# Layer-1 cross attention: keys and queries turned once and spread over the partitions by DMA, weighing in bursts

## The reference, cut to what matters

```python
q = split_heads(layernorm(latents) @ Wq)                 # [b, 16, 1024, 64]
k, v = split_heads(concat(latents, context) @ Wkv)       # [b, 16, 1101, 64]
q, k = rmsnorm(q) * qn_g, rmsnorm(k) * kn_g              # over the 64 of a head
attn = softmax(q @ k.T, masked)                          # [b, 16, 1024, 1101]
out = (attn @ v) @ Wout + bout                           # added to the residual
```

## Time and profile before

| | |
|---|---|
| median of 3 runs | 2421.39 us (2419.66 to 2424.4) |
| the profiled execution | 2413.85 us, span 2411.9 us |
| TensorE matmuls busy | 2050.4 us, 85% of the span |
| VectorE, ScalarE, GpSimd busy | 1344.9, 925.7 and 768.4 us (56%, 38%, 32%) |
| granted TensorE clock, mean | 0.925 |
| first and last exponential of layer 1's attention | 723.3 and 1943.7 us |

### The profile page before, as it was taken

One profiled execution on the slowest core, in us unless ns is written; L12 is line 12 of the kernel. 1 busy time (PEld: TensorE's weight loads), 2 busy tenths in 40 slices (PEclk: granted clock), 3 DMA queues, 4 the chain that ended last, 5 costly groups with the idle time before them and its releaser, 6 DMA issues. The chain is left out here.

```text
span 2411.9 us, 37994 instructions
## 1 busy us (share of the span) xinstructions
PE 2050.4 (85%) x12524; PEld 1558.7 (65%) x12525; DVE 1344.9 (56%) x3047; ACT 925.7 (38%) x1778; POOL 768.4 (32%) x730
## 2 busy tenths in 40 slices
PE   5889539997158999999999999999999934899993
PEld 3568535665046777777777877777777723567672
DVE  4371236665615777776777777767777725112223
ACT  3443202222124555544555555545554511222220
POOL 2200002332155444443454434544454100222220
PEclk9999759999559999999999999999999975899997
DMA  5512451111200000000000000000000055111113
GB/s 184 159 58 86 160 183 35 46 43 37 93 20 1 8 8 8 1 8 8 8 1 8 8 7 8 1 9 8 8 7 1 1 203 184 46 33 33 34 32 115
DMA packets 55772, 114.65 MB, mean 48 GB/s; under 512 B 8817, under 2 KB 41263, under 8 KB 53563
## 3 DMA queue, kind: packets, MB, share of 16 engines
q1 hardware_dynamic: 44987, 89.77, 10.6%
q0 software_dynamic: 8320, 20.65, 3.0%
q10 hardware_dynamic: 2304, 2.10, 0.3%
HBM read 79.90 MB, written 32.41 MB: 47 GB/s over the span
## 5 line engine op out<-in xcount | busy, mean ns | idle before, releaser
L1633 DVE TENSOR_REDUCE a_part_peak<-a_slot 128x1 f32<-128x512 f32 (+1 forms) x512 | 353.3, 728 | 124.3 <-PE a_slot L1467 121.4
L1467 PEld LDWEIGHTS a_slot<-a_KHL,a_QHL 128*128 128x128 f32 x1536 | 271.3, 190 | 176.8 <-issue 127.3
L1467 PE MATMUL a_slot<-a_KHL,a_QHL 128*128 128x512 f32 (+1 forms) x1536 | 342.9, 359 | 26.3 <-DVE a_probT L1663 12.8
L1492 PE MATMUL a_po<-a_probT,a_V 128*64 128x256 f32 (+1 forms) x2304 | 304.6, 390 | 3.3 <-DVE a_OT L1693 2.5
L1590 ACT ACTIVATE a_prob<-a_slot,a_npeak 128x1024 f32<-128x1024 f32 x256 | 284.5, 1111 | 1.3 <-DVE a_npeak L1635 1.2
L1663 DVE COPY a_probT<-a_slot 128x640 f32<-128x640 f32 x256 | 210.6, 823 | 102.8 <-PE a_slot L1476 92.7
L1476 PE MATMUL a_slot<-ident,a_prob 128*128 128x128 f32 x2048 | 265.4, 273 | 0.0
L1476 PEld LDWEIGHTS a_slot<-ident,a_prob 128*128 128x128 f32 x2048 | 231.7, 141 | 8.4
L1416 PE MATMUL a_side<-a_W,a_latT 128*128 128x128 f32 x1536 | 204.5, 289 | 21.0 <-issue 9.1
L1492 PEld LDWEIGHTS a_po<-a_probT,a_V 128*64 128x64 f32 (+1 forms) x2304 | 145.7, 136 | 92.1 <-issue 43.9
L1416 PEld LDWEIGHTS a_side<-a_W,a_latT 128*128 128x128 f32 x1536 | 188.2, 200 | 23.2 <-issue 9.5
(11 more groups left out here) (322 smaller groups left out, 3203.3 us busy)
## 6 DMA issues: line engine op xcount, KB each, us to landing
m_up<-_L_ffn_gate_up_proj_dram SPq DMA_DIRECT2D x8, 1024.0 KB
m_up<-in_L_ffn_W_dram SPq DMA_DIRECT2D x8, 1024.0 KB
m_down<-in_L_ffn_W_dram SPq DMA_DIRECT2D x8, 1024.0 KB
a_prob_dram<-a0p_zeros SPq DMA_DIRECT2D x4, 1632.0 KB, 10.6
a_dist_dram<-a_dist SPq DMA_DIRECT2D x4, 1632.0 KB, 8.2
a_band_prob<-a_prob_dram SPq DMA_DIRECT2D x4, 1632.0 KB, 6.7
a_W<-in_L_xattn_Wpair_dram SPq DMA_DIRECT2D x17, 384.0 KB, 3.1
m_bup<-_L_ffn_gate_up_bias_dram SPq DMA_DIRECT2D x1, 4096.0 KB
```

Source lines behind the costliest of these rows:

```text
L1467: ins = t_.matmul(out[:, lo:hi], q, KHL[:, pair.parity, h, part, lo:hi], start=part == 0, stop=part == 1)
L1492: ins = t_.matmul(po_t[h * D1:(h + 1) * D1, :], V[0:rows, pair.parity, j, h, :], probT[0:rows, gi % 2, j, h, :], start=j == PARTS[0][0], s ...
L1633: v.tensor_reduce(part[:, i:i + 1], slot[u % 2][:, lo:hi], AX.X, ALU.max).then_inc(part_peaked, 1)
```

## The change

- Keys and queries are scaled in place, once, and each tile is transposed once with both heads on its 128 rows. The high and low parts stand in new tiles `KT` and `QT`, head 0 on partitions 0 to 63, head 1 on 64 to 127.
- Four DMA transfers a pair copy `KT` to its places in `KHL`, and four for each half of the queries copy `QT` to `QHL`; each goes from 64 partitions to 64. SP issues them behind the weights' load. The scores wait for them.
- There are 12 pieces, in the units of `PIECE_OF`. In even units a piece stands behind the unit's transposes, in odd units at the unit's start.
- Weighing stands in odd units only, in parts of four and five tiles.
- VectorE now copies the first four tiles of the turned exponentials and ScalarE the other five, which waits for all nine.
- The bounds of the norms stand at the end of units 5 and 9.

```diff
-PARTS = [[8, 0], [1, 2], [3, 4], [5, 6, 7]]
-PIECES = ["Ka", "Kb", "c", "Qa", "Qb", "Va", "Vb", "K0a", "K0b", "K1a", "K1b", "Kc", "Q0a", "Q1a", "Q0b", "Q1b"]
-QUERY_TURNS = ["Q0a", "Q1a", "Q0b", "Q1b"]
-COPIED = ["Ka", "Kb", "c", "Qa", "Qb", "Va", "Vb"] + QUERY_TURNS
-SPLIT = [p for p in PIECES if p not in COPIED]
+PARTS = [[8, 0, 1, 2], [3, 4, 5, 6, 7]]
+PIECES = ["Ka", "Kb", "c", "Qa", "Qb", "Kta", "Va", "Ktb", "Ktc", "Qta", "Vb", "Qtb"]
+QUERY_TURNS = ["Qta", "Qtb"]
+SPLIT = ["Kta", "Ktb", "Ktc"]
+TURNED = SPLIT + QUERY_TURNS
+COPIED = [p for p in PIECES if p not in SPLIT]
+BOUND_AT = (5, 9)
+PIECE_OF = dict(zip([0, 2, 3, 4, 6, 7, 8, 9, 10, 11, 12, 13], PIECES))
...
-        kdup = sb("kdup", [P, KT_TILES, 2, 2, D1])
-        qdup = sb("qdup", [P, S, 2, 2, D1])
+        KT = sb("KT", [P, 2, KEYS], F32R)
+        QT = sb("QT", [P, 2, SEQ], F32R)
...
+            def spread_keys(pair):
+                sp.wait_ge(dve_freed, count(pair, "Ktc", SPLIT))
+                for h in range(2):
+                    for half in range(2):
+                        sp.dma_start(KHL[half * D1:(half + 1) * D1, pair.parity, h, :, 0:KEYS].bitcast(F32),
+                                     KT[h * D1:(h + 1) * D1, :, :].bitcast(F32)).then_inc(k_spread, 16)
+            def spread_queries(pair, k):
+                sp.wait_ge(qlow, pair.g * 2 + (k + 1))
+                for h in range(2):
+                    for part in range(2):
+                        sp.dma_start(QHL[part * D1:(part + 1) * D1, pair.parity, h, k * BANK:(k + 1) * BANK].bitcast(F32),
+                                     QT[h * D1:(h + 1) * D1, part, k * BANK:(k + 1) * BANK].bitcast(F32)).then_inc(q_spread[k], 16)
             def body(pair):
                 if not isinstance(pair.g, int) or pair.g + 2 < BATCH * PAIRS:
-                    sp.wait_ge(filled, count(pair, PIECES[-1], PIECES))
+                    sp.wait_ge(filled, count(pair, "Vb", PIECES))
                     load_weights((pair.hp + 2) % PAIRS if isinstance(pair.g, int) else pair.hp + 2, pair.parity)
+                spread_keys(pair)
+                for k in range(2):
+                    spread_queries(pair, k)
...
+                    x = nat[:, :, :].rearrange("p t (h d) -> p (t h) d", h=2)
+                    g_.tensor_tensor(x, x, inv[:, :].unsqueeze(2).to_broadcast([P, 2 * tiles, D1]), ALU.mult).then_inc(scaled, 1)
+                for k, step in enumerate(QUERY_TURNS):
+                    cols = slice(k * BANK, (k + 1) * BANK)
                     if not first:
-                        pool.wait_ge(filled, count(Pair(pair.g - 1, 0, 0, 0), last, PIECES))
-                    for h in range(2):
-                        src = nat[:, :, h * D1:(h + 1) * D1]
-                        scale = inv[:, :].rearrange("p (t h) -> p t h", h=2)[:, :, h:h + 1].to_broadcast([P, tiles, D1])
-                        for d in range(2):
-                            ins = g_.tensor_tensor(dup[:, :, h, d, :], src, scale, ALU.mult)
-                    ins.then_inc(scaled, 1)
-                for k, step in enumerate(QUERY_TURNS):
-                    lo = BANK if step.endswith("b") else 0
+                        pool.wait_ge(q_spread[k], n * 64)
                     pool.wait_ge(act_freed, count(pair, step, COPIED))
-                    q = QHL[:, pair.parity, int(step[1]), lo:lo + BANK]
-                    g_.tensor_tensor(q, qgam[:, k % 2, :], one[:, :].to_broadcast([P, BANK]), ALU.mult).then_inc(qhigh, 1)
-                    pool.wait_ge(qhigh, n * 4 + (k + 1))
-                    g_.tensor_tensor(q[D1:, :], qgam[D1:, k % 2, :], q[D1:, :], ALU.subtract).then_inc(qlow, 1)
-                    pool.wait_ge(qlow, n * 4 + (k + 1))
+                    g_.tensor_tensor(QT[:, 0, cols], qgam[:, k, :], one[:, :].to_broadcast([P, BANK]), ALU.mult).then_inc(qhigh, 1)
+                    pool.wait_ge(qhigh, n * 2 + (k + 1))
+                    g_.tensor_tensor(QT[:, 1, cols], qgam[:, k, :], QT[:, 0, cols], ALU.subtract).then_inc(qlow, 1)
...
-                    pe.wait_ge(dve_freed, count(pair, "Kc", SPLIT))
-                if u % 2 == 0 and t % HALF == 0:
-                    pe.wait_ge(qlow, count(pair, QUERY_TURNS[h + t // HALF * 2], QUERY_TURNS))
+                    pe.wait_ge(k_spread, (pair.g + 1) * 64)
+                if u % (UNITS // 2) == 0:
+                    pe.wait_ge(q_spread[u // (UNITS // 2)], (pair.g + 1) * 64)
...
-                    if after:
-                        piece(after, PIECES[u])
+                    if after and u % 2 == 1 and PIECE_OF.get(u):
+                        piece(after, PIECE_OF[u])
                     pe.wait_ge(exped, pair.g * UNITS + (u + 1))
                     if u % 2 == 1 and two_before[0]:
                         project_outputs(*two_before, u // 2 % 2)
                     if u % 4 == 2 and one_before[0]:
                         turn_sums(*one_before)
                     turn(pair, u)
-                    if one_before[0]:
-                        weigh(*one_before, u % 4)
+                    if after and u % 2 == 0 and PIECE_OF.get(u):
+                        piece(after, PIECE_OF[u])
+                    if one_before[0] and u % 2 == 1:
+                        weigh(*one_before, u // 2 % 2)
...
-            def copy_first(pair, u):
-                act.wait_ge(turned, (pair.g * UNITS + u) * 3 + 2)
+            def copy_rest(pair, u):
+                one_before, two_before = group_before(pair, u, 1), group_before(pair, u, 2)
+                if u % 2 == 1 and two_before[0]:
+                    act.wait_ge(added, (two_before[0].g * GROUPS + two_before[1]) * 2 + (u // 2 % 2 + 1))
+                if u % 4 == 2 and one_before[0]:
+                    act.wait_ge(r_out, one_before[0].g * GROUPS + (one_before[1] + 1))
+                act.wait_ge(turned, (pair.g * UNITS + u) * 3 + 3)
                 t, h = tile_head(u)
-                a_.activation(probT[:, u // 4 % 2, 0:HALF, h, u % 2 * P:(u % 2 + 1) * P],
-                              slot[u % 2][:, 0:HALF * P].rearrange("p (t q) -> p t q", q=P), ACT.Copy).then_inc(probT_act, 1)
+                a_.activation(probT[:, u // 4 % 2, HALF:KT_TILES, h, u % 2 * P:(u % 2 + 1) * P],
+                              slot[u % 2][:, HALF * P:KT_TILES * P].rearrange("p (t q) -> p t q", q=P), ACT.Copy).then_inc(probT_act, 1)
...
-            def bound(pair, step):
-                if step in ("Qb", "K0b"):
-                    j = int(step == "K0b")
+                    lo = {"Kta": 0, "Ktb": BANK, "Ktc": SEQ}[step]
+                    hi = min(lo + BANK, KEYS)
+                    v.tensor_tensor(KT[:, 1, lo:hi], side[:, 0:hi - lo], KT[:, 0, lo:hi], ALU.subtract).then_inc(dve_freed, 1)
+            def bound(pair, j):
                     var = (kvar, qvar)[j]
                     dve.wait_ge(summed, pair.g * (2 * FOLDS) + (j + 1) * FOLDS)
                     sums = square[:, 0:(KT_TILES, S)[j], :].rearrange("p t (h d) -> p (t h) d", h=2)
                     v.tensor_scalar(var[:, :], sums[:, :, 0], D1 * 1e-16, None, ALU.max).then_inc(bounded, 1)
-            def copy_rest(pair, u):
-                dve.wait_ge(turned, (pair.g * UNITS + u) * 3 + 3)
+            def copy_first(pair, u):
+                dve.wait_ge(turned, (pair.g * UNITS + u) * 3 + 2)
                 t, h = tile_head(u)
-                v.tensor_copy(probT[:, u // 4 % 2, HALF:KT_TILES, h, u % 2 * P:(u % 2 + 1) * P],
-                              slot[u % 2][:, HALF * P:KT_TILES * P].rearrange("p (t q) -> p t q", q=P)).then_inc(probT_dve, 1)
+                v.tensor_copy(probT[:, u // 4 % 2, 0:HALF, h, u % 2 * P:(u % 2 + 1) * P],
+                              slot[u % 2][:, 0:HALF * P].rearrange("p (t q) -> p t q", q=P)).then_inc(probT_dve, 1)
...
-                    if after:
-                        piece(after, PIECES[u])
+                    if after and u % 2 == 1 and PIECE_OF.get(u):
+                        piece(after, PIECE_OF[u])
                     if u % 2 == 1 and two_before[0]:
                         dve.wait_ge(turned, (pair.g * UNITS + u) * 3 + 1)
                         add_outputs(*two_before, u // 2 % 2)
                     if u % 4 == 2 and one_before[0]:
                         dve.wait_ge(turned, (pair.g * UNITS + u) * 3 + 1)
                         copy_sums(*one_before)
-                    copy_rest(pair, u)
+                    copy_first(pair, u)
                     row_sum(pair, u)
                     if u % 4 == 3:
                         invert(pair, u // 4)
                     nxt = ahead(pair, u, 2)
                     if nxt[0]:
                         peak(*nxt)
-                    if after:
-                        bound(after, PIECES[u])
+                    if after and u % 2 == 0 and PIECE_OF.get(u):
+                        piece(after, PIECE_OF[u])
+                    if after and u in BOUND_AT:
+                        bound(after, BOUND_AT.index(u))
```

(38 more changed lines are left out.)

11 lines of the change are left out of this document (3 added, 8 removed).

## The result

The changed kernel takes 2657.13 us in the median of 4 runs (2653.92 to 2667.2), against 2420.52 for the kernel before: a ratio of 1.0975, 95% interval 1.0947 to 1.1003. I forecast 2598, in 2490 to 2655: slower was right, and so was the place of each wait, but the time lies 59 us above the forecast and 2 us above the range.

The account below looks back on a forecast made before the run. TensorE's own work was taken to bound the stage. A pair gained +11.3 us from removed work, three waits and lower clock: 170 over 15 hand-overs plus 7 for the last, from 2421 to 2598 us; range 2490 to 2655.

Parts of the forecast that it names:

- wait for the keys' scale: TensorE in unit 7, at the keys' transposes, waits for GpSimd's scaling: 2.76 us a pair.
- wait for the queries' scale: TensorE in unit 11, at the queries' transposes, waits for GpSimd's scaling: 3.21 us a pair.
- wait for the spread: TensorE at unit 14's score waits for SP's DMA transfers: 6.4 us a pair, less 0.15 of idle absorbed.
- parts 1 to 3: TensorE's halved transposes, remaining work and added idle: a pair takes 73.30 us without the waits, 2.52 less than before.
- part 6: TensorE's steps after the long DMA wait run at lower clock: 1.61 us a pair; nothing for waits under 3.5.
- rival (d): Every TensorE wait halves the clock too: 3.2 us a pair on top, 2646 us; chance 0.08.
- part 5: Key and query transfers queue behind SP's weights load; 2.779 MB at 240 GB/s delays unit 14's score 6.4 us.
- Parts 4 and 3: TensorE waits 2.76 and 3.21 us for GpSimd's scaling; lost cover around ScalarE's copy, units 10 and 14, adds 1.83 idle.
- Part 2: TensorE's work after: 71.47 us a pair; the old pair's 2.29 of small waits, chiefly for the copy, all go.
- Part 7: The ends: last pair, without pieces, costs 7 us more; prologue nothing net.
- Rival (c): Faster: removed work decides if TensorE's three waits total under 2.1 us a pair; 2390 us with none; chance 0.09.

Follow-up runs that it names:

- the 2372 us kernel: The kernel with both edits, small key piece copied on ScalarE before the exponentials and split on VectorE before the peaks: 2372.22 us, ratio 0.9819.
- The filled kernel: The changed kernel, waits kept, TensorE turning the identity 18 times before each scale wait and 56 before the spread wait: 2607.27 us, ratio 1.0779.
- the first experiment: The changed kernel, with SP sending keys and first half of queries when ready, before waiting for Vb and loading weights: 2507.83 us, ratio 1.0368.
- the early bounds: The changed kernel, with the norms bounded at the end of units 4 and 8 instead of 5 and 9: 2560.08 us, ratio 1.0584.
- 2348 us: The 2372 us kernel, with weighing of units 9 to 15 in three parts and four parts in the last pair: 2348.07 us, ratio 0.9680.
- the kernel with both edits: The changed kernel, with the spread sent ahead of the weights and the bounds in units 4 and 8: 2406.2 us, ratio 0.9949.

## Why the prediction was right in kind and short in size

I set the terms a pair against a middle pair of the trace after:

| term | forecast | measured | from |
|---|---|---|---|
| work and idles without the waits | 73.30 | 72.3 | the pair of the 2372 us kernel, parts 1 to 3 |
| wait for the keys' scale | 2.76 | 2.78 | 1520.63 + 1.16 to 1524.57 |
| wait for the queries' scale | 3.21 | 2.8 | scaling took 1.90 and not 2.06, unit 10 0.2 longer |
| wait for the spread | 6.25 | 7.7 | turn 14 to score 9.71; 2.04 without the wait |
| lower clock | 1.61 | 6.9 | below |
| sum | 87.1 | 92.5 | the trace: 92.6, 1481.40 to 1574.00, score behind the spread to the next |

**The step that failed is part 6**, and with it the sentence "For waits under 3.5 I add nothing". I had one passage behind a wait of 7.51, priced two steps of it, and let the short waits go free; they stood only in rival (d), at 0.08. What the rows after show: behind the keys' wait (2.6) projection, turn and weighing take 0.72, 2.05 and 2.67, where 0.43, 1.07 and 2.31 are normal: 1.6. Behind the queries' wait, by the same steps and the transposes (0.89): 2.6. Behind the spread's, the score 2.13, the projection 0.99, the turn 2.06, the weighing 2.58, where 1.16, 0.51 (it stands behind a score here), 1.07 and 2.31 are normal: 2.7. The turns stand wholly at the lower level of 1.2 GHz, against 2.4 elsewhere (granted clock 0.50 and 1.00); in some of the other steps the clock changes. Over the whole trace such passages stand behind the keys' wait in 13 of 15 pairs (21 in all), behind the queries' in all 15 (35) and behind the spread's in all 14 (36): 6.1 in the mean of the 15 hand-overs, against the 1.61 of the sum. The filled kernel took the first two away and left the waits, which shows that the clock is a cost of its own. Rival (d) had this mechanism; had I put it into the sum with the price of 1.61 each, the forecast would have been 2646, still 11 short, since the slow passages are longer than that behind two of the three waits.

**The spread (part 5)** was in its place, and its rate a little under the 240 that I took: about 225 in the mean of the stage rows, which makes 12.4 of transfers and not 11.6. The page "SBUF — State Buffer" of the Trainium skill, "Door 1: The DMA port swizzle (why [64,N] ≈ [32,N])", gives 218 GB/s for 64 partitions and 436 for 128. The trace comes near it, with 225 in the mean for 64, 3% above the page's figure, and 411 to 421 for 128 once the weights are out of the way. I kept it out of the sum since no row of before showed it; it would have given a wait of 7.5, an estimate, and 7.7 was measured. SP's order, the cause that the transfers start so late, is shown by the first experiment.

**Parts 4 and 3** held to 0.4. For part 4 the early bounds are the proof; they also uncovered the next wait in line, the split of Ktc behind the peaks, which I had not named. It lay hidden in the wait for the queries' scale.

**Part 2** got its size by the wrong reason. I called the 2.29 of the old pair small waits for copies. The list of waits of before has only 12.8 for this copy over 740 to 1940, 0.8 a pair. A good part of the rest goes by the order of the work, which the bursts and the projections ahead of the scores improve with no wait in play; the kernel that weighs in every unit shows it. That the term was nearly right in size was luck. The gain was larger than I let it be, 3.5 a pair with the transposes, not 2.52.

**Part 7.** From the first projection of the stage to unit 0's score (674.6 and 735.02 before, 683.7 and 751.09 after) the prologue costs 7, where I said nothing net: TensorE waits 14.6 there for the first spread. The last pair costs 5.3 from its first turn to its last sums, not 7. The 15 hand-overs cost 230 by the two traces (1151.6 and 1381.7 between these points), 15.3 each where the sum had 11.3. These 4.0 a hand-over are nearly the whole error, and by the table and the mean of the clock they come from about 4.5 for the clock and 1.3 for the spread too little, and 0.4 for the queries' scale and 1.0 for the work too much. (The two profiled executions lie 253 apart, the medians 237: that of after began the stage 9 later, in code that is the same.)

Rival (c), faster, was refuted for the change as it stands: it needed the three waits under 2.1 a pair, and they are 13.3. That the removed work is worth something once they are gone is also shown: 2372 and 2348 us.

## What to carry to other kernels

Where an engine is busy 99% of a stage, halving one of its parts gains a few per cent, and each new wait in its queue can cost more than its length: here 2.8 with 1.4 of slow steps, 2.8 with 2.3, and 7.7 with 2.6, in the mean. For every step that is moved, look where the producer's own chain begins (here a bound behind the peaks of a unit, a transfer behind an unrelated load), not only at how long it is. A copy over 64 partitions should be priced at half of the rate over 128 (225 against 411 to 421 GB/s here), and issued as soon as its data are there.

## What was not expected of the hardware

- Idles of 0.90 and 1.31, with one score between them, brought the steps behind to the lower clock in some pairs and not in others of the same execution (6 of 15 with idles of this kind in the kernel with both edits, 10 of 15 with only the bounds moved). Behind the two waits for the scales in the changed kernel (2.1 to 2.7 each) it was 28 of 30. Idles of 0.8 to 1.3 in units 10 and 14, without the wait for the split, left the steps of unit 11 at full speed in all 15 pairs. What decides between two pairs with the same idles, no run shows.
- 18 or 56 transposes of the identity in a wait keep the steps behind it at full speed: in all 15 pairs behind each wait for a scale, in 8 of 14 behind the spread's. In 4 of 15 pairs the 18 in front of the queries' scale ran slow themselves.
- The order of matmul work alone moves its price: 16 weighing matmuls take 1.88 in one burst and 2.03 in two, a projection 1.70 ahead of a score and 1.88 ahead of weighing, with no wait in the profile.
- With the keys' and queries' transfers queued one behind the other, an issue of one key transfer holds SP for 1.8 in the median and 0.6 at least; the four of the keys took 5.99.
